# Two gelus ahead of the present pair's high half: a reordering on ScalarE in a four-layer mixture-of-experts kernel

## The reference

```python
def _moe_layer(x, rw, rb, g, b, w1, b1, w2, b2):
    logits = jnp.einsum('bsh,he->bse', x, rw) + rb
    probs = jax.nn.softmax(logits, axis=-1)
    vals, idx = jax.lax.top_k(probs, K)
    vals = vals / vals.sum(axis=-1, keepdims=True)
    ...
    xe = xhat[None] * g[:, None, None, :] + b[:, None, None, :]
    h = jax.nn.gelu(jnp.einsum('ebsh,ehf->ebsf', xe, w1) + b1[:, None, None, :], approximate=False)
    y = jnp.einsum('ebsf,efh->ebsh', h, w2) + b2[:, None, None, :]
    expert_out = x[None] + y
    comb = jnp.einsum('bsk,bske->bse', vals, jax.nn.one_hot(idx, E, dtype=x.dtype))
    return jnp.einsum('bse,ebsh->bsh', comb, expert_out)
```

## Time and profile before

| | before |
|---|---|
| time, median of 3 runs | 1749.76 us (1746.67 to 1753.34) |
| time of the profiled execution | 1748.56 us |
| its span on the core | 1746.5 us |
| TensorE busy | 1501.3 us, 86% |
| VectorE busy | 1299.8 us, 74% |
| ScalarE busy | 1231.0 us, 70% |
| GpSimd busy | 875.5 us, 50% |

### The profile page before, as it was taken

One profiled execution on the slowest core, in us unless ns is written; L12 is line 12 of the kernel. 1 busy time (PEld: TensorE's weight loads), 2 busy tenths in 40 slices (PEclk: granted clock), 3 DMA queues, 4 the chain that ended last, 5 costly groups with the idle time before them and its releaser, 6 DMA issues. The chain is left out here.

```text
span 1746.5 us, 39659 instructions
## 1 busy us (share of the span) xinstructions
PE 1501.3 (86%) x11654; PEld 1179.6 (68%) x11654; DVE 1299.8 (74%) x4048; ACT 1231.0 (70%) x2137; POOL 875.5 (50%) x1434
## 2 busy tenths in 40 slices
PE   7899999843329999989999998999999898888882
PEld 4556655533227888878888887878888787766761
DVE  6989999833337888778888887888888787666662
ACT  4445444211139888878888887888888788999992
POOL 1111111155543555645555554555555457788776
PEclk9999999955559999999999999999999999999996
DMA  3899820012246667656676675567767556766651
GB/s 91 304 404 405 340 65 12 20 62 80 69 146 201 217 209 233 222 182 201 194 223 214 199 239 184 182 195 239 212 210 234 187 192 174 188 180 179 184 137 8
DMA packets 196044, 323.96 MB, mean 185 GB/s; under 512 B 47789, under 2 KB 127999, under 8 KB 195872
## 3 DMA queue, kind: packets, MB, share of 16 engines
q1 hardware_dynamic: 168608, 298.46, 52.0%
q0 software_dynamic: 27264, 23.54, 6.0%
HBM read 218.99 MB, written 108.71 MB: 188 GB/s over the span
## 5 line engine op out<-in xcount | busy, mean ns | idle before, releaser
L1071 DVE TENSOR_TENSOR hl<-hg,hh 128x1024 fp32r<-128x1024 f32 x336 | 409.2, 1221 | 221.1 <-ACT hh L996 221.1
L990 ACT ACTIVATE hg<-ps_h,bb 128x512 f32<-128x512 f32 x672 | 438.4, 684 | 136.2 <-PE ps_h L1343 133.6
L904 POOL DMA_INDIRECT regions<-nrow,posi x316 | 358.0, 1133 | 139.7 <-issue 76.8
L996 ACT ACTIVATE hh<-hg 128x1024 fp32r<-128x1024 f32 x336 | 355.2, 1057 | 2.8
L1341 PE MATMUL ps_h<-xTh,w1b 128*128 128x512 f32 x672 | 288.6, 429 | 2.1 <-DVE xTl L1087 1.4
L1343 PE MATMUL ps_h<-xTh,w1b 128*128 128x512 f32 x672 | 266.8, 397 | 0.0
L1342 PE MATMUL ps_h<-xTl,w1b 128*128 128x512 f32 x672 | 266.3, 396 | 0.0
L1358 PE MATMUL ps_y<-hh,w2b 128*128 128x512 f32 x672 | 266.1, 396 | 0.0
L1356 PE MATMUL ps_y<-hh,w2b 128*128 128x512 f32 x672 | 265.3, 395 | 0.0
L1357 PE MATMUL ps_y<-hl,w2b 128*128 128x512 f32 x672 | 264.6, 394 | 0.0
L1372 PE MATMUL ps_q<-ir,yb 128*128 128x140 f32 (+2 forms) x1008 | 152.8, 284 | 22.5 <-DVE nrow L1108 13.9
(11 more groups left out here) (197 smaller groups left out, 2643.2 us busy)
## 6 DMA issues: line engine op xcount, KB each, us to landing
w1b<-w_split SPq DMA_DIRECT2D x168, 512.0 KB, 4.3
w2b<-w_split SPq DMA_DIRECT2D x168, 512.0 KB, 4.2
regions<-zero SPq DMA_DIRECT2D x98, 582.0 KB, 12.8
row<-regions SPq DMA_DIRECT2D x84, 294.0 KB, 4.4
w_split<-wst SPq DMA_DIRECT2D x32, 512.0 KB, 5.2
wr<-in_L_ffn_w_dram SPq DMA_DIRECT2D x32, 256.0 KB, 4.6
regions<-nrow,posi POOLq DMA_INDIRECT x316, 3.0
x<-in_L_attn_x_dram SPq DMA_DIRECT2D x16, 256.0 KB, 2.9
```

What stands on the lines that cost most here:

```text
L904: g.indirect_dma_start(out=regions[layer % 2], out_offset=bass.IndirectOffsetOnAxis(ap=posi[r % 2][:, b:b + 1], axis=0), in_=nrow[r % 2][: ...
L990: a.activation(hg[c // 2 % PAIRS][:, c % 2 * TILE:(c % 2 + 1) * TILE], ps_h[c % BANKS][:], ACT.Gelu, bias=bb[n % 4][k // FC][:, k % FC:k % ...
L996: a.activation(hh[j % PAIRS][:], hg[j % PAIRS][:], ACT.Identity).then_inc(hi, 1)
L1071: v.tensor_tensor(hl[n][:], hg[n][:], hh[n][:].bitcast(F32), ALU.subtract).then_inc(lo, 1)
```

## The change

In each quarter ScalarE did the high half of the present pair and then the two gelus of the next pair. It now does the two gelus first.

```diff
                     for j in range(KT // 2):
                         if i < N:
-                            high(i * (KT // 2) + j)
                             for c in range(2):
                                 if i * KT + 2 * j + 2 + c < N * KT:
                                     gelu(i * KT + 2 * j + 2 + c)
+                            high(i * (KT // 2) + j)
                         if j == 0:
                             if i + 1 < N:
                                 x_high(i + 1)
```

## The result

The changed kernel took 2121.63 us (median of 4 runs, 2117.69 to 2125.74) against 1748.22 us (median of 4) for the kernel before on the same chip: a ratio of 1.213, with a 95% interval of 1.2093 to 1.2168. It is 373 us slower; forecast were 2119 us, in a range of 2055 to 2205.

The account below looks back on a forecast made before the run. TensorE was taken to bound the steps, so its waits add to the time. 1748.56 us profiled + 301 (layers 0 to 2) + 31 (last layer) + 38 (clock) = 2119 us, range 2055 to 2205.

Parts of the forecast that it names:

- the layer ends: Three steps at the ends of layers 0 to 2 wait for the next layer's rows; 3 x 5.2 = 15.6 us stays.
- the clock: TensorE, layers 0 to 2: clock falls behind waits in 6 of 10 steps, 1.0 us each, +38 us.
- The three waits: Layers 0 to 2, each step: `y_tokens` second part waits 2.42 us, third part 1.94, `count` 0.70; step 18.67 us.
- VectorE's list as the carrier: VectorE's update, routing and `stats` behind each late rest wait with it, and TensorE waits for those; 5.06 us a step.
- Last layer: Last layer's 17 steps: third part of `y_tokens` 1.82 us later, containing the second part's new wait; +31 us.
- Banks: Rival: each `ps_h` bank is emptied 0.96 us earlier, so TensorE gains time; 1718 us, chance 0.04.
- No change: Rival: the 6 us of lead before `second` absorbs one pair on ScalarE; 1750 us, chance 0.03.
- only the first wait: Rival: only `y_tokens`' second part waits, as ScalarE and VectorE get ahead for the step's rest; 1881 us, chance 0.06.
- The heavy clock: Rival: TensorE's clock stays low much of the time, falling at both waits of a step; 2269 us, chance 0.07.

Follow-up runs that it names:

- the kernels of single quarters: Four kernels, each the kernel before with ScalarE's new order in only one quarter, 0 to 3: 1950.67, 1915.49, 1867.18 and 1748.56 us.
- the kernels with the rests last: VectorE's rest of each quarter moved behind that quarter's other work: 1744.4 us with ScalarE's new order (from the changed kernel), 1722.78 with the old (from the kernel before).
- filling the waits: Changed kernel with six more TensorE matmuls ahead of the second and of the third part of `y_tokens`: 2085.08 us, ratio 1.1929 to the kernel before.
- quarter 3: Kernel before with ScalarE's new order in quarter 3 only: 1748.56 us, ratio 1.0005.
- quarter 1 alone: Kernel before with ScalarE's new order in quarter 1 only: 1915.49 us, ratio 1.0973.
- quarter 0 alone: Kernel before with ScalarE's new order in quarter 0 only: 1950.67 us, ratio 1.1156.
- one rest last: Changed kernel with VectorE's rest of quarter 0 alone behind that quarter's other work: 1987.4 us, ratio 1.1361 to the kernel before.

## Why the prediction was right

The mechanism and its sizes held in the full change. That the total came within 3 us of 2121.63 is in part luck: the layer ends were put 6 us too high and the clock 4 too low.

- *The three waits.* Worked out 4.33, 3.85 and 6.48 us from the end of a chunk; measured 4.34 (1409.04 - 1404.70), 3.87 (1414.52 - 1410.65) and, from chunk 7's end at 1415.89 (its gelu starts at 1415.92), 6.40 for `count`. The step without a fall of the clock: 18.67 us worked out, 18.67 measured. That the second and third wait would not be swallowed by the first is shown by the step and by the kernels of single quarters.
- *VectorE's list as the carrier.* Shown by the kernels with the rests last: 377 us come back with ScalarE's order unchanged.
- *Layer ends.* 5.2 us each were kept; the three steps took 22.36, 21.20 and 22.02 us, on average 3.2 above the 18.67 of a step without a fall. So 15.6 should have been 9.5: the wait for the next layer's rows, 3.2 to 3.5 us before, is 0.9 to 2.3 now.
- *The clock.* 38 us were forecast, as 38 falls of 1.0 us. There were 50; the steps lose 1246.6 - 64 x 18.67 - 9.5 = 42 us, 0.84 each, and filling the waits gave 38 back. The sum was right by two errors against each other. A fall is cheaper here than in the single quarters, where it cost 1.5 to 1.6 us and the allowance was too small, since the slow work takes up part of the third part's wait: that is 1.80 us in a step without a fall, but 87.3 us in 66 times, 1.3 on average, in the whole.
- *Last layer.* 31 us forecast, 31.5 measured. The third part waits 1.81 us as before; the second part waits 1.78 more. A usual step grew by 1.98 us (14.35 to 16.33) and not by 1.82, and the two falls that this layer had before are gone.
- *The rivals.* Banks: the wait of a chunk's first matmul for `hg` was 0.2 us, and no kernel with the new order and VectorE's list as it was is faster than before. No change and only the first wait: refuted by the waits. The heavy clock: 0.93, not near one half.

What was wrong was said of parts: that quarter 3 costs something alone, and that with the rests last the order would not matter.

## What to carry to other kernels

When an instruction is moved later on one engine, look at what stands behind its consumer on the consumer's engine, not only at the consumer's own deadline: `second` had 6 us in hand, but the update behind the rest had 0.15. An engine that waits in order should do first what others wait for soonest; putting the rests behind the updates on VectorE made the kernel 1.4% faster with no other change. A margin near zero in the trace between a producer and the bounding engine is where the price of a reordering is read.

## What the hardware showed that was not expected

TensorE's clock fell to the 1.2 GHz level more often where the regular wait was longer: 0 falls in the 17 last-layer steps with waits of 1.78 and 1.81 us (the changed kernel), 19 in 64 steps with 1.80 to 1.83 us (quarter 1 alone), 38 in 64 with 2.27 to 2.30 us and longer ones at the layers' ends (quarter 0 alone), 14 in 17 with 2.44 us and more (quarter 1 alone, last layer), and one in each of 17 with 3.4 us (one rest last). But the length is not all: of the 19 falls in quarter 1 alone, 16 lie in the first 21 steps and 3 in the other 43, with nearly the same wait. What else decides was not tested. In the changed kernel each of the 50 falls began within 1.7 us of the end of a wait of 1.8 us or more. Multiplying into a bank that is overwritten afterwards, 1.4 us of each wait, removed 48 of 50 falls and made the kernel 37 us faster.
